# Eight products with the high half of x first, then the four with its low halves, in the first score of each masked phase

## The reference, cut to what matters

```
q = x @ Wq;  k = ctx @ Wk;  v = ctx @ Wv           # 16 heads of 64
logits = q k^T / 8 + bias[token, key]
probs = softmax(logits)
x = x + (probs v) @ Wo + bo
```

## Time and profile before

| | |
|---|---|
| median of 3 runs | 1506.82 us (1506.38 to 1507.56) |
| the profiled execution | 1507.22 us, of which the span of the trace is 1505.4 us |
| TensorE (PE) busy | 1484.9 us, 99% of the span |
| VectorE, GpSimd (POOL), ScalarE (ACT) busy | 991.4, 911.1, 745.4 us |
| mean granted TensorE clock | 0.998 of full speed |

### The profile page before, as it was taken

One profiled execution on the slowest core, in us unless ns is written; L12 is line 12 of the kernel. 1 busy time (PEld: TensorE's weight loads), 2 busy tenths in 40 slices (PEclk: granted clock), 3 DMA queues, 4 the chain that ended last, 5 costly groups with the idle time before them and its releaser, 6 DMA issues.

```text
span 1505.4 us, 24275 instructions
## 1 busy us (share of the span) xinstructions
PE 1484.9 (99%) x8992; PEld 1213.9 (81%) x8992; DVE 991.4 (66%) x1644; ACT 745.4 (50%) x1317; POOL 911.1 (61%) x825
## 2 busy tenths in 40 slices
PE   7998999999999999999999999999999999999998
PEld 7987887888778877888788877887788877887787
DVE  5676757765776657665776667565766577666764
ACT  4565675335732564346633573346533663357321
POOL 0084477557765587567756686468756776568541
PEclk9999999999999999999999999999999999999999
DMA  9999563122322231132212232133113231222101
GB/s 331 328 400 408 198 233 92 43 85 78 127 56 66 99 120 51 43 126 85 80 46 74 92 113 64 34 136 120 43 43 105 79 101 54 65 99 92 57 1 56
DMA packets 101652, 170.17 MB, mean 113 GB/s; under 512 B 17056, under 2 KB 51360, under 8 KB 95520
## 3 DMA queue, kind: packets, MB, share of 16 engines
q1 hardware_dynamic: 97552, 151.06, 30.1%
q10 hardware_dynamic: 3824, 17.04, 2.8%
q0 software_dynamic: 160, 0.53, 0.1%
HBM read 116.95 MB, written 51.65 MB: 112 GB/s over the span
## 4 chain that ended last, share of the span: by engine, by line
PE 89%; POOL 3%; ACT 2%; DVE 2%; DMA 1%; issue 1%; SPq 1%; ACTq 0%; DVEq 0%
PE OB L383 17%; PE OB L384 16%; PE OB L385 16%; PE SB L383 10%; PE SB L385 9%; PE SB L384 9%; POOL xhl L1368 3%; PE TB L531 3%; PE MX L506 2%; PE TB L506 2%; PE TB L568 1%; DMA s_fm<-prob 1%; PE SB L491 1%; PE OB L438 1%; PE OB L435 1%
## 5 line engine op out<-in xcount | busy, mean ns | idle before, releaser
L1339 POOL TENSOR_TENSOR prob<-prob,small 128x512 f32<-128x512 f32 x256 | 278.8, 1092 | 254.5 <-DVE small L1139 254.3
L836 ACT ACTIVATE prob<-prob 128x512 f32<-128x512 f32 x128 | 80.8, 632 | 270.9 <-DVE prob L1126 270.2
L1117 DVE SCALAR_TENSOR_TENSOR prob<-SB,aux 128x512 f32<-128x512 f32 x128 | 88.1, 688 | 181.4 <-PE SB L385 180.8
L1333 POOL TENSOR_TENSOR prob<-prob,small 128x512 f32<-128x512 f32 x128 | 136.4, 1066 | 117.1 <-DVE small L1111 117.1
L383 PE MATMUL SB<-foldM,xhl 128*128 128x512 f32 x512 | 203.8, 398 | 2.5 <-POOL xhl L1368 1.4
L383 PE MATMUL OB<-pT,foldN 128*128 128x512 f32 x512 | 205.1, 401 | 0.0
L384 PE MATMUL OB<-pT,foldN 128*128 128x512 f32 x512 | 200.0, 391 | 0.0
L385 PE MATMUL OB<-pT,foldN 128*128 128x512 f32 x512 | 199.8, 390 | 0.0
L385 PE MATMUL SB<-foldM,xhl 128*128 128x512 f32 x512 | 199.8, 390 | 0.0
L384 PE MATMUL SB<-foldM,xhl 128*128 128x512 f32 x512 | 199.4, 390 | 0.0
L1111 DVE TENSOR_REDUCE small<-prob 128x8 f32<-128x512 f32 x128 | 87.1, 680 | 91.2 <-ACT prob L846 90.2
(11 more groups left out here) (144 smaller groups left out, 3879.0 us busy)
## 6 DMA issues: line engine op xcount, KB each, us to landing
prob<-in_wkvM_dram SPq DMA_DIRECT2D x32, 512.0 KB, 8.0
ring<-s_fm SPq DMA_DIRECT2D x64, 256.0 KB, 5.3
ring<-s_fn SPq DMA_DIRECT2D x128, 128.0 KB, 2.6
out_dram<-x ACTq DMA_DIRECT2D x15, 1024.0 KB, 3.9
s_fm<-prob SPq DMA_DIRECT2D x16, 512.0 KB, 9.2
wraw<-in_wqG_dram SPq DMA_DIRECT2D x8, 1024.0 KB, 7.0
s_fn<-x SPq DMA_DIRECT2D x16, 512.0 KB, 5.6
ring<-in_xT_dram SPq DMA_DIRECT2D x32, 256.0 KB, 3.1
```

The lines of the kernel that those rows point to most:

```text
L836: act.activation(own, own, ACT.Exp).then_inc(S["exped"], 1)
L1117: dve.scalar_tensor_tensor(out=own, in0=bank, scalar=M_SCALE, in1=row, op0=ALU.mult, op1=ALU.add).then_inc(S["biased"], 1)
L1333: pool.tensor_tensor(own, own, hmax[u % 2].unsqueeze(2).broadcast_to([P, HH, KEYS]), ALU.subtract).then_inc(S["evac"], 1)
L1339: pool.tensor_tensor(own, own, rsum[u % 2].unsqueeze(2).broadcast_to([P, HH, KEYS]), ALU.mult).then_inc(S["normed"], 1)
```

## The change

In phases 2 and 3, at u = 0 only, the loop over the four chunks is split in two. First come, for each chunk, the two products that use the high half of x (high with high, high with low of foldM), which wait for `xb_hi` of that chunk and for `fa_lo`. Then come the four products with the low half of x, each with its own wait for the low half of its chunk. The same twelve products go into the same bank. All other scores are as they were.

```diff
                     e = 2 * it + ph - 2
-                    for c in range(DC):
-                        if u == 0:
+                    if u == 0:
+                        for c in range(DC):
+                            pe.wait_ge(S["xb_hi"], 4 * e + c + 1)
+                            pe.wait_ge(S["fa_lo"], 4 * it + c + 1)
+                            pe.matmul(out[:, :], xhl[:, 0, c, tok], foldM[:, 0, c, 0:HALF], start=(c == 0), stop=False)
+                            pe.matmul(out[:, :], xhl[:, 0, c, tok], foldM[:, 1, c, 0:HALF], start=False, stop=False)
+                        for c in range(DC):
                             if c == 2:
                                 pe.wait_ge(S["xb_lo_d"], e + 1)
                             else:
                                 pe.wait_ge(S["xb_lo_p"], 3 * e + min(c, 2) + 1)
-                            pe.wait_ge(S["fa_lo"], 4 * it + c + 1)
+                            last = pe.matmul(out[:, :], xhl[:, 1, c, tok], foldM[:, 0, c, 0:HALF],
+                                             start=False, stop=(c == DC - 1))
+                    for c in range(DC if u else 0):
                         if u == 4:
                             pe.wait_ge(S["fb_lo"], 12 * it + c + 1)
                         last = three(out[:, :], xhl[:, 0, c, tok], xhl[:, 1, c, tok],
```

## The result

Five runs of the changed kernel have a median of 1498.86 us (1497.77 to 1500.46), five of the kernel before 1506.82 us (1505.62 to 1507.69): 7.96 us less, a ratio of 0.9949 with a 95% interval of 0.9938 to 0.9960. A second set on another occasion gave 1500.53 us (6 runs) against 1506.32 us (29 runs), ratio 0.9959 (0.9945 to 0.9973). The change is faster; 1500.5 us had been predicted.

A forecast was written before the change was run, and what follows sets the result against it. TensorE was taken to bound the kernel. Over 8 iterations, 0.46 us (phase 2) plus 0.34 us (phase 3) gave 3.7 + 2.7 = 6.4 us, so 1500.5 us was predicted, with a range of 1498.8 to 1503.2 us.

The forecast's parts named there:

- The bound: Whole kernel: TensorE is busy 1484.9 of 1505.4 us, so only what makes TensorE stop is worth anything.
- Phase 2, 0.46 us: First score of phase 2: next work starts at 406.78, not 407.24, gaining 0.46 of 0.80 us lost per iteration.
- Phase 3, 0.34 us: First score of phase 3: all low halves in time, score takes 2.72 us against 3.06, gaining 0.34 us per iteration.
- The tight wait: Phase 3, chunk 3's low half: in time with 0.19 us to spare; rival that it is missed, 1502.1 us, chance 0.08.
- No giving back: Later TensorE waits take nothing back; rival that they take all or most of the gain, 1505 to 1507 us, chance 0.10.
- Met waits at nothing: 64 new met waits in 16 scores cost 0 to 1.3 us, taken as 0; restart rival 1510.2 us, chance 0.04.
- The price of the pace: Two matmul slots in phase 2: 0.46 us at the trace's 227 ns, 0.26 us at the skill's 131 ns.

The follow-up runs named there:

- phase 2 alone: The new order in phase 2 only, phase 3 left as in the kernel before: 1502.70 us, ratio 0.9976 to the kernel before.
- this half of the change: The new order in phase 3 only, phase 2 left as in the kernel before: 1503.85 us, ratio 0.9979 to the kernel before.
- The run with VectorE's half later: Changed kernel, but in phase 2 VectorE makes chunk 2's low half after the first ot_lo; low products go 0, 1, 3, 2: 1501.43 us, ratio 0.9965 to before.
- 1300 of them: Changed kernel, with every matmul of all other masked scores also waiting for the long-met fa_lo: 1498.28 us, ratio 0.9949 to the kernel before.
- a single wait for all: Changed kernel, but the first low product waits for all four low halves at once: 1510.90 us against 1506.85, ratio 1.0025 to the kernel before.

## Why the prediction was right

**The bound.** TensorE sets the time, and only its gaps count. Right: 6.3 us of gaps gone are 6.3 us of the stretch.

**Phase 2, 0.46 us.** The wait for chunk 3 was to stay, with its own matmul alone to come and not three. Measured 0.44 us (3.64 less 3.20) in iterations 1 to 7, a score of 3.20 us where 3.17 had been forecast; the stretch of phase 2 alone gives 3.7 us, as the sum had it. In iteration 0 the score starts sooner by 0.34 us after the work ahead of it, since there the first wait for a low half had been late; the prediction had not looked at iteration 0 by itself. The total there is nearly the same, 0.43 us from the work ahead of the score to the work behind it, since the score still ends on GpSimd's third half.

**Phase 3, 0.34 us.** Measured 0.34 (3.06 less 2.72), and 2.8 us for this half of the change. The tight wait held: GpSimd ends 2.07 us after the score's start in this trace as well, ahead of the 2.27 at which it is needed, and the spare time stayed between 0.15 and 0.2 us in all eight iterations. The run with VectorE's half later shows why it had a margin at all: GpSimd's third half meets no subtraction of VectorE's in phase 3 and takes 1.29 us.

**No giving back.** VectorE's idle time ahead of the last evacuation of phase 2 is 0.40 us after the change, against 0.41: the whole chain moved with TensorE, as argued. One reading of the prediction was wrong here: 0.41 us is the least idle time that the view of waits shows, and not the least there is. Of the 16 evacuations of that iteration two follow VectorE's own work with no idle time and one with 0.07 us, before and after the change alike. They took nothing back either, since VectorE's work ahead of them hangs on earlier scores and moves too; the iteration is 0.8 us shorter.

```profile
434.01 0.69 DVE L1124 SCALAR_TENSOR_TENSOR prob<-SB,aux 128x512 f32<-128x512 f32 x1 [0.40 <-PE SB L385]
```

**Met waits at nothing.** Right, and now with 1300 of them.

**The price of the pace.** The 131 ns that the Trainium skill gives ("TensorE: Matmul & The Clock Gate", section "Back-to-back issue gap") would have made phase 2's part 2.1 us; it is 3.7, so the 227 ns of the trace were the ones to use.

**What was off.** The median of the first set is 1.6 us under the forecast of 1500.5, which is within what executions of one kernel differ by in their opening (234.76 against 237.49 us in the changed kernel's two traces), and that the second set's 1500.53 falls on the forecast is luck. The sum itself (6.4 us) is met within 0.1 us by the stretch. The prediction called 0.4 us the distance between the profiled execution and the median and took the rest of the spread for nothing; the runs of the kernel before lie between 1502.88 and 1510.75.

## What to carry to other kernels

Where one accumulation takes operands that become ready one after another, let each product wait only for what it uses, and put those whose operands come last at the end: what counts is how much work stands behind the last late wait, and work that uses another bank can be put ahead of that wait as well. Met waits cost nothing that these runs could see on TensorE, so it pays to wait as late and as finely as possible; a single wait for all threw the gain away and 3.5 us besides. Whether the fine waits would have done it without the new order was not run. A change of 6 us in 1500 is read best from two fixed matmuls in the trace, between which two executions of the same kernel differed by 0.2 us, where its whole times differed by up to 8.

## What the runs showed of the hardware

- In these trains a matmul of 512 columns with its weight load runs at 0.227 us from start to start; one whose weight load had to wait costs 0.11 us more, and the load follows the release by 0.05 us (0.11 in the kernel with one wait for all).
- VectorE's and GpSimd's subtractions of two SBUF operands (128x512, float32) do not overlap: the later one ends 0.55 us (VectorE) or 1.13 to 1.17 us (GpSimd) after the other has finished, for three different starts of VectorE's, and its recorded duration includes the wait (1.04 and 1.48 us, 1.76 us).
- The granted clock of TensorE between 16 and 22 us is 0.72 in some executions and 1.00 in others, of either kernel, with 38 or 40 matmuls there in place of 53.
